# Linear attention on one core: block matrix held stationary, one reciprocal over the whole tile, the low halves of the turned rows on GpSimd

## The chip, the core and the metric

The kernel runs on one core of a Trainium2 chip. The metric is the device time of one execution in microseconds (us), taken as the median over runs of the same kernel.

## What is computed

Four stages act one after another on x of shape (8, 256, 1024): a linear attention against a context, a feed-forward net with 4-bit weights, an autocorrelation attention and a low-rank layer. The change touches the first stage and what it hands to the second:

```python
def _layernorm(x, axis=-1, eps=1e-05): ...

def _L0_xattn_ref(q, k, v):              # B, C, N = 8, 256, 1024; H = 8 heads of dh = 32
    ...
    qh = jax.nn.softmax(qh, axis=3)      # over the 32 channels of a head
    kh = jax.nn.softmax(kh, axis=1)      # over the 1024 positions
    kvs = jnp.einsum('bnhd,bnhe->bhde', kh, vh)
    out = jnp.einsum('bnhd,bhde->bnhe', qh, kvs)
    return out.transpose(0, 2, 3, 1).reshape(B, C, N)

x = x + jnp.tanh(g_xattn[0]) * _L0_xattn_ref(_layernorm(x, axis=-1), ctx_4096, ctx_4096)
x = x + jnp.tanh(g_ffn[0]) * _L0_ffn_ref(_layernorm(x, axis=-1), ...)
```

## The kernel before

The first stage is `phase_linear_attention`. It works on 16 tiles, each of 128 rows (channels) by 1024 columns (positions), in float32; a tile holds four heads of 32 rows. All 16 tiles of x stay in the tile X. Each engine has a program of its own, written out by hand: a function `step(i, h)` that is run for i from 0 to 18, with `exists` leaving out what lies before the first or behind the last tile. The engines are tied by semaphores alone, and most buffers are double (index h). An instruction that waits holds back all that stands behind it on its engine.

For tile i the work is this.

- VectorE (`prepare`) takes the mean and variance of the rows of X and the maximum of the context rows; GpSimd (`rsqrt`, lines 389 to 394) makes the reciprocal root from the variance, and VectorE the offset (line 538).
- ScalarE makes the exponentials of the queries (line 419, eq) and of the keys (line 425, ek).
- TensorE turns ek with eight transposes into psE (line 488), and sums eq over the 32 rows of each head into psB (line 494): there the data are the stationary operand and the block matrix blk, of ones in four 32 by 32 blocks, is the moving one, so psB holds the sums turned, and each sum 32 times. VectorE takes the reciprocal of every 32nd column, 32 in all (line 562, rS). ScalarE spreads them over 1024 columns into rSx (line 454), TensorE turns that back into psB (line 512), ScalarE copies psB to rSx (line 461), and GpSimd multiplies eq by it (line 401).
- ScalarE copies the turned keys (line 448, ekT), TensorE multiplies them with the context (line 507), VectorE masks and scales the product (line 579, kvm), TensorE multiplies with eq (line 501, psO), and VectorE adds the result to X (line 567). This last pair is done one step later, at step i + 1.
- Still at step i + 1, VectorE takes mean and variance of the new row of X (line 530), GpSimd the root, and ScalarE writes the normalised rows to xn (line 471). xn lies in two buffers, one of `wt` and one of `absm`.
- At step i + 2 TensorE turns xn into psX (line 518) and ScalarE writes its high half in 16 bits to z (line 430, `turned_high`). At step i + 3 VectorE writes the low half, psX minus the high half (line 552, `turned_low`).

ScalarE also does a part of the next phase's weight decoding between these (line 442). The end of the phase has a small chain of scales for the feed-forward net (`ffn_scales`), run for the last steps: its power on GpSimd is line 200. After the phase all engines meet, and the feed-forward net begins.

Of the kernel before, what the change touches and what calls it, by code (L numbers as in the profile page):

```python
# [22 lines left out]
ALU = mybir.AluOpType  # L23
# [3 lines left out]
P = 128  # L27
# [258 lines left out]
def phase_linear_attention(nc, io, res):  # L286
# [9 lines left out]
    with ExitStack() as ctx:  # L296
# [7 lines left out]
        c_in, cT, eq, ek, ekT = (sb(n, [P, D]) for n in ("c_in", "cT", "eq", "ek", "ekT"))  # L304
        xn = [t.rearrange("p a b -> p (a b)") for t in (res["wt"][:, 2:4, :], res["absm"][:, 0:2, :])]
        spare = parts(res["made"][:].rearrange("p a b -> p (a b)").bitcast(F32))
        kvm, rS, st, st2 = ([spare(n) for h in range(2)] for n in (P, D // ROWS0, 12, 12))
        spare = parts(res["made"][:].rearrange("p a b -> p (a b)").bitcast(F32)[:, 4 * P - 48:])
        mv, mv2, ve, rstd, nmr, ve2, rstd2, nmr2, cm, ncm, ksum, rks = ([spare(n) for h in range(2)] for n in (2, 2, *(1,) * 10))
        rSx = res["wt"][:, 0:2, :].rearrange("p a b -> p (a b)")  # L310
# [6 lines left out]
        mv_done, rstd_done, nmr_done = (sem(n) for n in ("mv_done", "rstd_done", "nmr_done"))  # L317
        cmax_done, ncm_done, eq_done, ek_done, rks_done = (sem(n) for n in ("cmax_done", "ncm_done", "eq_done", "ek_done", "rks_done"))
        ekT_mm, ekT_done, kv_mm, kvm_done = (sem(n) for n in ("ekT_mm", "ekT_done", "kv_mm", "kvm_done"))
        sums_mm, rS_done, rSx_done, rS_mm, eqn_done, out_mm, x_done = (sem(n) for n in ("sums_mm", "rS_done", "rSx_done", "rS_mm", "eqn_done", "out_mm", "x_done"))  # L320
        mv2_done, rstd2_done, nmr2_done = (sem(n) for n in ("mv2_done", "rstd2_done", "nmr2_done"))
        turned_done = sem("turned_done")
        hi_done = res["hi_done"]
# [5 lines left out]
        def halves_of(i, h):  # L329

            b, r = i // 2, i % 2
            return x_tiles(res, b // QUARTS)[:, :, r, b % QUARTS, h]

        def turned_bank():
            return psX[:].rearrange("p (f k t) -> p f k t", f=2, k=KD // 2)
# [12 lines left out]
        with nc.Block() as block:  # L348
# [38 lines left out]
            @block.gpsimd  # L387
            def _(pool):
                def rsqrt(i, h, mv_, ve_, rs_, mvd, rsd):
                    pool.wait_ge(mvd, 3 * i + 3)  # L390
                    settle(pool)
                    pool.tensor_scalar(ve_[h][:], mv_[h][:, 1:2], EPS, None, ALU.add).then_inc(rsd, 1)
                    pool.wait_ge(rsd, 2 * i + 1)
                    pool.tensor_tensor(rs_[h][:], ve_[h][:], mhalf[:], ALU.pow).then_inc(rsd, 1)

                def step(i, h):
                    if exists(i - 1):
                        rsqrt(i - 1, 1 - h, mv2, ve2, rstd2, mv2_done, rstd2_done)
                    if exists(i):
                        pool.wait_ge(turned_done, i + 1)  # L400
                        pool.tensor_tensor(eq[h][:], rSx[:], eq[h][:], ALU.mult).then_inc(eqn_done, 1)
                    if exists(i + 2):
                        rsqrt(i + 2, h, mv, ve, rstd, mv_done, rstd_done)

                pool.memset(mhalf[:], -0.5).then_inc(const_set, 1)
                pool.memset(res["half"][:], 0.5).then_inc(const_set, 1)
                pool.memset(res["ones"][:], 1.0).then_inc(const_set, 1)
                pool.wait_ge(const_set, 3)
                for h in range(2):
                    rsqrt(h, h, mv, ve, rstd, mv_done, rstd_done)  # L410
                run(pool, step, scales_pool)

            @block.scalar
            def _(act):
                def query_exponentials(i, h):
                    act.wait_ge(nmr_done, i + 1)
                    after(act, out_mm, i - 1)
                    settle(act)
                    act.activation(eq[h][:], X[:, i, :], ACT.Exp, scale=rstd[h][:], bias=nmr[h][:]).then_inc(eq_done, 1)

                def key_exponentials(i, h):
                    after(act, ekT_mm, i - 1)
                    after(act, rks_done, i - 1)
                    act.wait_ge(ncm_done, i + 1)
                    act.activation(ek[h][:], c_in[h][:], ACT.Exp, bias=ncm[h][:], accum_out=ksum[h][:]).then_inc(ek_done, 1)

                def turned_high(i):
                    act.wait_ge(xT_mm, i + 1)
                    settle(act)
                    act.activation(halves_of(i, 0), turned_bank(), ACT.Copy, scale=LN_SCALE).then_inc(hi_done, 1)  # L430

                def first_kinks(i):

                    turn, k = divmod(i - 1, len(kinks))
                    if 0 <= turn < 2:
                        scale, bias, alpha = kinks[k]
                        act.wait_ge(res["first_in"], 16 * (AHEAD // 2) * (turn + 1))
                        if k:
                            act.wait_ge(res["kink_done"], AHEAD // 2 * (i - 1))
                        for u in range(AHEAD // 2 * turn, AHEAD // 2 * (turn + 1)):  # L440
                            block_u = res["first"][:, u, :]
                            act.activation(block_u, block_u if k else block_u.bitcast(I32), ACT.Prelu, bias=bias, scale=scale, alpha=alpha).then_inc(res["kink_done"], 1)

                def step(i, h):
                    if exists(i):
                        after(act, kv_mm, i - 1)
                        act.wait_ge(ekT_mm, i + 1)
                        act.activation(ekT[h][:], psE[:], ACT.Copy).then_inc(ekT_done, 1)
                    first_kinks(i)
                    if exists(i):  # L450
                        after(act, eqn_done, i)
                        act.wait_ge(rS_done, i + 1)

                        act.activation(rSx[:].rearrange("p (n r) -> p n r", r=ROWS0), rS[h][:].unsqueeze(2).to_broadcast([P, D // ROWS0, ROWS0]),
                                       ACT.Copy).then_inc(rSx_done, 1)
                    if exists(i + 1):
                        query_exponentials(i + 1, 1 - h)
                        key_exponentials(i + 1, 1 - h)
                    if exists(i):
                        act.wait_ge(rS_mm, i + 1)  # L460
                        act.activation(rSx[:], psB[:], ACT.Copy).then_inc(turned_done, 1)
                    if i == 0:
                        act.wait_ge(bound_in, 32)
                        act.activation(tg[:], gates[:], ACT.Tanh).then_inc(tanh_done, 1)
                    if i == TILES:
                        turned_high(i - 2)
                    if exists(i - 1):
                        after(act, xT_mm, i - 2)
                        act.wait_ge(nmr2_done, i)
                        settle(act)  # L470
                        act.activation(xn[1 - h][:], X[:, i - 1, :], ACT.Identity, scale=rstd2[1 - h][:], bias=nmr2[1 - h][:]).then_inc(xn_done, 1)
                    if exists(i - 2) and i != TILES:
                        turned_high(i - 2)

                act.wait_ge(const_set, 2)
                act.activation(rstd2[0][:], res["half"][:], ACT.Exp)
                key_exponentials(0, 0)
                query_exponentials(0, 0)
                run(act, step, scales_act)

            @block.tensor
            def _(pe):
                def step(i, h):
                    if exists(i):
# [3 lines left out]
                            mm = pe.transpose(psE[:, k * P:(k + 1) * P], ek[h][:, k * P:(k + 1) * P], ident[:])  # L488
                        mm.then_inc(ekT_mm, 1)

                        after(pe, turned_done, i)
                        pe.wait_ge(eq_done, i + 1)
                        for k in range(KD):
                            mm = pe.matmul(psB[:, k * P:(k + 1) * P], eq[h][:, k * P:(k + 1) * P], blk[:], start=True, stop=True)
                        mm.then_inc(sums_mm, 1)
                    if exists(i - 1):
                        pe.wait_ge(eqn_done, i)
# [5 lines left out]
                    if exists(i):  # L503
# [3 lines left out]
                            mm = pe.matmul(psE[:, 0:P], ekT[h][:, k * P:(k + 1) * P], cT[h][:, k * P:(k + 1) * P], start=(k == 0), stop=(k == KD - 1))  # L507
                        mm.then_inc(kv_mm, 1)

                        pe.wait_ge(rSx_done, i + 1)  # L510
                        for k in range(KD):
                            mm = pe.transpose(psB[:, k * P:(k + 1) * P], rSx[:, k * P:(k + 1) * P], ident[:])
                        mm.then_inc(rS_mm, 1)
                    if exists(i - 2):
                        pe.wait_ge(xn_done, i - 1)
                        after(pe, lo_done, i - 2)
                        for k in range(KD):
                            mm = pe.transpose(psX[:, k * P:(k + 1) * P], xn[h][:, k * P:(k + 1) * P], ident[:])
                        mm.then_inc(xT_mm, 1)
# [5 lines left out]
            def _(dve):  # L525
# [21 lines left out]
                    dve.wait_ge(cmax_done, i + 1)  # L547
                    dve.tensor_scalar(ncm[h][:], cm[h][:], -1.0, None, ALU.mult).then_inc(ncm_done, 1)

                def turned_low(i):  # L550
                    dve.wait_ge(hi_done, i + 1)
                    dve.scalar_tensor_tensor(halves_of(i, 1), turned_bank(), LN_SCALE, halves_of(i, 0), ALU.mult, ALU.subtract).then_inc(lo_done, 1)

                def step(i, h):
                    if exists(i - 3) and i != TILES + 1:
                        turned_low(i - 3)
                    if exists(i):
                        dve.wait_ge(ek_done, i + 1)
                        dve.reciprocal(rks[h][:], ksum[h][:]).then_inc(rks_done, 1)
                        dve.wait_ge(sums_mm, i + 1)  # L560

                        dve.reciprocal(rS[h][:], psB[:, 0:D:ROWS0]).then_inc(rS_done, 1)
                    if exists(i - 1):
                        dve.wait_ge(out_mm, i)
                        if i == 1:
# [5 lines left out]
                        stats(i - 1, 1 - h, st2, mv2, mv2_done)  # L571
                        if i == TILES:
                            scales_dve(dve, "every")
                            turned_low(i - 2)
                    if exists(i):
                        dve.wait_ge(rks_done, i + 1)
                        dve.wait_ge(kv_mm, i + 1)
# [2220 lines left out]
```

## Time and profile before

| | |
|---|---|
| median of 3 runs | 1982.77 us (1982.44 to 1983.53) |
| profiled execution, own time | 1984.28 us |
| its span, first to last instruction | 1982.5 us |
| TensorE busy in the span | 1925.9 us, 97% |
| VectorE, ScalarE, GpSimd busy | 1268.0, 1248.0, 822.3 us |
| mean granted TensorE clock | 0.992 |
| linear attention phase | the first 176 us or so |

The page gives busy times for the whole span; what the change can do has to be read from the phase that it touches. That phase repeats one pattern per tile, so two neighbouring steps of the timeline, and the start of the same instruction in each, give the length of a step. In the rows a tile that lies in another's memory bears that one's name: `made` holds the small vectors (statistics, offsets, rS, kvm), `wt` holds rSx and one of the two xn, `absm` the other xn, `z` the turned halves. PEld is the loading of weights into TensorE. A float32 matmul appears as two matmul records.

### The profile page before, as it was taken

How to read it: one execution, taken by the hardware profiler on the slowest of the kernel's cores; microseconds unless marked ns; L12 is line 12 of the kernel's file. 1: busy time of each engine (PE TensorE's matmuls, PEld its weight loads, DVE VectorE, ACT ScalarE, POOL GpSimd, SP SyncE). 2: the span in 40 equal slices, each digit the busy share in tenths (PEclk: the TensorE clock that was granted, in tenths of full speed). 3: DMA queues.
4: the chain of work that ended last, by engine and by line, in shares of the span. 5: the costliest groups of instructions: out<-in, count | busy, mean ns of one | idle time of the engine just before them, and what ended most of it. 6: DMA issues, size and time to landing. Idle time of an engine off the chain costs nothing. (4 is left out here: it accounts for less than half of the span.)

```text
span 1982.5 us, 26463 instructions
## 1 busy us (share of the span) xinstructions
PE 1925.9 (97%) x9188; PEld 969.2 (49%) x9188; DVE 1268.0 (64%) x2184; ACT 1248.0 (63%) x1989; POOL 822.3 (41%) x746
## 2 busy tenths in 40 slices
PE   7996999999999999999999999999999899999998
PEld 6773444444444444444444444444444455555544
DVE  6776666573645747365463745546389888888872
ACT  6885888667876777676777767765534444344431
POOL 3433644532222232232322323222278667767742
PEclk9997999999999999999999999999999999999999
DMA  6641733248566383765737465562551110111001
GB/s 222 204 164 54 245 99 96 104 169 284 196 212 233 113 279 110 241 202 168 262 102 269 145 222 200 159 246 77 202 165 32 33 53 24 47 54 38 27 22 43
DMA packets 89972, 288.33 MB, mean 145 GB/s; under 512 B 11760, under 2 KB 16496, under 8 KB 72944
## 3 DMA queue, kind: packets, MB, share of 16 engines
q1 hardware_dynamic: 89840, 286.64, 42.8%
q8 instruction: 74, 1.21, 0.3%
q14 instruction: 58, 0.48, 0.1%
HBM read 259.33 MB, written 27.26 MB: 145 GB/s over the span
## 5 line engine op out<-in xcount | busy, mean ns | idle before, releaser
L1050 ACT ACTIVATE first<-first 128x512 f32<-128x512 f32 (+1 forms) x1024 | 635.9, 626 | 26.3 <-DVE wt L1459 1.8
L1284 POOL TENSOR_TENSOR gu<-wt,gu 128x512 f16<-128x512 f32 x86 | 102.5, 1192 | 389.5 <-ACT gu L1071 389.5
L1459 DVE SCALAR_TENSOR_TENSOR wt<-first,w_scale,absm 128x512 f32<-128x512 f32 x132 | 102.3, 775 | 237.8 <-ACT first L1050 237.3
L1806 PE MATMUL a_psQ<-z,gu 128*128 128x512 f16 x840 | 187.2, 379 | 0.0
L2409 PE MATMUL a_psL<-z,l_x 128*128 128x512 f16 x768 | 170.7, 379 | 1.0 <-DVE l_x L2511 0.8
L1806 PE MATMUL a_psC<-z,gu 128*128 128x512 f16 x660 | 151.3, 379 | 0.0
L1806 PE MATMUL a_psC<-z 128*128 128x512 f16 x612 | 140.4, 379 | 0.0
L1462 DVE SCALAR_TENSOR_TENSOR wt<-a_psE,lora_gain,wt 128x512 f32<-128x512 f32 x132 | 99.1, 751 | 54.0 <-PE a_psE L1764 26.9
L1806 PEld LDWEIGHTS a_psQ<-z,gu 128*128 128x128 f16 x840 | 82.2, 98 | 99.1
L1284 POOL TENSOR_TENSOR dn_lo<-wt,dn_hi 128x512 f16<-128x512 f32 x42 | 49.0, 1167 | 192.1 <-ACT dn_hi L1071 192.1
L1296 POOL TENSOR_TENSOR hid_lo<-z,hid_hi 128x512 f16<-128x512 f32 x68 | 80.6, 1199 | 109.7 <-ACT hid_hi L1112 109.6
L1071 ACT ACTIVATE gu<-wt 128x512 f16<-128x512 f32 x86 | 53.5, 622 | 105.1 <-DVE wt L1462 81.3
L2409 PEld LDWEIGHTS a_psL<-z,l_x 128*128 128x128 f16 x768 | 74.9, 98 | 89.0 <-issue 1.2
L1521 DVE SCALAR_TENSOR_TENSOR X<-a_psL,ffn_gain,X 128x512 f32<-128x512 f32 x132 | 95.3, 745 | 24.5 <-PE a_psL L1863 24.4
L1284 POOL TENSOR_TENSOR z<-wt,z 128x512 f16<-128x512 f32 x51 | 59.8, 1188 | 103.2 <-ACT z L1071 103.2
L1863 PE MATMUL a_psL<-dn_hi,hid_hi 128*128 128x512 f16 x268 | 101.6, 379 | 0.2 <-DVE X L1521 0.2
L1863 PE MATMUL a_psL<-dn_hi,hid_lo 128*128 128x512 f16 x268 | 101.5, 379 | 0.0
L1521 DVE SCALAR_TENSOR_TENSOR X<-a_psQ,ffn_gain,X 128x512 f32<-128x512 f32 x106 | 77.7, 746 | 36.6 <-PE a_psQ L1863 36.6
L1806 PEld LDWEIGHTS a_psC<-z,gu 128*128 128x128 f16 x660 | 63.8, 98 | 74.2
L1521 DVE SCALAR_TENSOR_TENSOR X<-a_psC,ffn_gain,X 128x512 f32<-128x512 f32 x108 | 78.8, 746 | 32.6 <-PE a_psC L1863 32.6
L1863 PE MATMUL a_psL<-dn_lo,hid_hi 128*128 128x512 f16 x254 | 96.2, 379 | 0.0
L1806 PEld LDWEIGHTS a_psC<-z 128*128 128x128 f16 x612 | 59.5, 98 | 70.5
(421 smaller groups left out, 4180.5 us busy)
## 6 DMA issues: line engine op xcount, KB each, us to landing
z<-x_parts SPq DMA_DIRECT2D x126, 1024.0 KB, 5.8
first<-in_codes SPq DMA_DIRECT2D x132, 256.0 KB, 3.1
absm<-in_absmax SPq DMA_DIRECT2D x264, 128.0 KB, 3.4
c_in<-in_ctx SPq DMA_DIRECT2D x16, 512.0 KB, 5.1
X<-in_x SPq DMA_DIRECT2D x16, 512.0 KB, 4.8
cT<-in_ctxT SPq DMA_DIRECT2D x16, 512.0 KB, 3.5
o_sp<-in_w SPq DMA_DIRECT2D x16, 512.0 KB, 4.4
z<-in_ctx SPq DMA_DIRECT2D x8, 1024.0 KB, 7.2
```

The source lines that it names most:

```text
L1050: act.activation(level[w % 2][:], codes[w % RING] if k == 0 else level[w % 2][:], ACT.Prelu, bias=bias, scale=scale, alpha=alpha).then_inc ...
L1071: act.activation(dest(c, name, 0), wt[slot(name)], ACT.Copy).then_inc(whi_done, 1)
L1284: pool.tensor_tensor(low, source, high, ALU.subtract).then_inc(wlo_done, 1)
L1296: pool.tensor_tensor(low, buf, high, ALU.subtract).then_inc(hidlo_done, 1)
L1459: dve.scalar_tensor_tensor(wt[at], source[:], w_scale[:, m:m + 1], absm[w % RING][:], ALU.mult, ALU.mult).then_inc(scaled, 1)
L1462: dve.scalar_tensor_tensor(wt[at], ps_lora[w % 2], lora_gain[:, m:m + 1], wt[at], ALU.mult, ALU.add).then_inc(wt_done, 1)
L1521: dve.scalar_tensor_tensor(dst, ps_ring[down_bank(j, n)], ffn_gain[:], dst, ALU.mult, ALU.add).then_inc(acc_done, 1)
L1806: mm = pe.matmul(out, w[:, k * P:(k + 1) * P], xx[:, k], start=first and q == 0, stop=q == 3 * KD // 2 - 1, skip_group_check=True)
L1863: mm = pe.matmul(ps_ring[down_bank(j, n)], hh[c][:, i * P:(i + 1) * P], w[c][:, hf * BANK:(hf + 1) * BANK], start=(q == 0), stop=(q == len ...
L2409: mm = pe.matmul(sum_bank(d, half), a[:, ks], w[:, k, half * CB:(half + 1) * CB], start=(q == 0), stop=(q == 3 * KD - 1))
```

## The change

The matmuls at line 494 become two matmuls of 512 columns, with blk stationary and eq moving, so that psB holds the sums in the layout of eq. VectorE takes the reciprocal of all 1024 columns of psB straight into rSx, and GpSimd multiplies by that. The 32 column reciprocal, ScalarE's spreading, the eight transposes and ScalarE's copy fall away. The turned rows are first copied by ScalarE from psX into the memory of xn (`turned_rows`); ScalarE then makes the high half from this copy, and the low half becomes a subtraction on GpSimd of operands in SBUF, at the end of GpSimd's step. The wait ahead of writing xn (line 468) is now for the low half of the tile that used this buffer before, and no longer for its transposes.

```diff
@@ gpsimd
+                def turned_low(i):
+                    pool.wait_ge(hi_done, i + 1)
+                    pool.tensor_tensor(halves_of(i, 1), turned_rows(i), halves_of(i, 0), ALU.subtract).then_inc(lo_done, 1)
+
                 def step(i, h):
                     if exists(i - 1):
                         rsqrt(i - 1, 1 - h, mv2, ve2, rstd2, mv2_done, rstd2_done)
                     if exists(i):
-                        pool.wait_ge(turned_done, i + 1)
+                        pool.wait_ge(rS_done, i + 1)
                         pool.tensor_tensor(eq[h][:], rSx[:], eq[h][:], ALU.mult).then_inc(eqn_done, 1)
                     if exists(i + 2):
                         rsqrt(i + 2, h, mv, ve, rstd, mv_done, rstd_done)
+                    if exists(i - 3):
+                        turned_low(i - 3)
@@ scalar
                 def turned_high(i):
                     act.wait_ge(xT_mm, i + 1)
                     settle(act)
-                    act.activation(halves_of(i, 0), turned_bank(), ACT.Copy, scale=LN_SCALE).then_inc(hi_done, 1)
+                    act.activation(turned_rows(i), turned_bank(), ACT.Copy, scale=LN_SCALE).then_inc(turned_done, 1)
+                    act.wait_ge(turned_done, i + 1)
+                    act.activation(halves_of(i, 0), turned_rows(i), ACT.Copy).then_inc(hi_done, 1)
...
-                    if exists(i):
-                        after(act, eqn_done, i)
-                        act.wait_ge(rS_done, i + 1)
-
-                        act.activation(rSx[:].rearrange("p (n r) -> p n r", r=ROWS0), rS[h][:].unsqueeze(2).to_broadcast([P, D // ROWS0, ROWS0]),
-                                       ACT.Copy).then_inc(rSx_done, 1)
                     if exists(i + 1):
                         query_exponentials(i + 1, 1 - h)
                         key_exponentials(i + 1, 1 - h)
-                    if exists(i):
-                        act.wait_ge(rS_mm, i + 1)
-                        act.activation(rSx[:], psB[:], ACT.Copy).then_inc(turned_done, 1)
...
                     if exists(i - 1):
-                        after(act, xT_mm, i - 2)
+                        after(act, lo_done, i - 2)
@@ tensor
-                        after(pe, turned_done, i)
+                        after(pe, rS_done, i)
                         pe.wait_ge(eq_done, i + 1)
-                        for k in range(KD):
-                            mm = pe.matmul(psB[:, k * P:(k + 1) * P], eq[h][:, k * P:(k + 1) * P], blk[:], start=True, stop=True)
+                        for n in range(2):
+                            mm = pe.matmul(psB[:, n * BANK:(n + 1) * BANK], blk[:], eq[h][:, n * BANK:(n + 1) * BANK], start=True, stop=True)
                         mm.then_inc(sums_mm, 1)
...
-                        pe.wait_ge(rSx_done, i + 1)
-                        for k in range(KD):
-                            mm = pe.transpose(psB[:, k * P:(k + 1) * P], rSx[:, k * P:(k + 1) * P], ident[:])
-                        mm.then_inc(rS_mm, 1)
                     if exists(i - 2):
                         pe.wait_ge(xn_done, i - 1)
-                        after(pe, lo_done, i - 2)
+                        after(pe, turned_done, i - 2)
@@ vector
-                def turned_low(i):
-                    dve.wait_ge(hi_done, i + 1)
-                    dve.scalar_tensor_tensor(halves_of(i, 1), turned_bank(), LN_SCALE, halves_of(i, 0), ALU.mult, ALU.subtract).then_inc(lo_done, 1)
-
                 def step(i, h):
-                    if exists(i - 3) and i != TILES + 1:
-                        turned_low(i - 3)
                     if exists(i):
                         dve.wait_ge(ek_done, i + 1)
                         dve.reciprocal(rks[h][:], ksum[h][:]).then_inc(rks_done, 1)
                         dve.wait_ge(sums_mm, i + 1)
 
-                        dve.reciprocal(rS[h][:], psB[:, 0:D:ROWS0]).then_inc(rS_done, 1)
+                        after(dve, eqn_done, i)
+                        dve.reciprocal(rSx[:], psB[:]).then_inc(rS_done, 1)
...
                             scales_dve(dve, "every")
-                            turned_low(i - 2)
```

## Rows read from the trace of the kernel before

**Rows 1.** The page: busy time of each engine, share of the span, instructions
```profile
PE 1925.9 (97%) x9188; PEld 969.2 (49%) x9188; DVE 1268.0 (64%) x2184; ACT 1248.0 (63%) x1989; POOL 822.3 (41%) x746
```

**Rows 2.** Stretches: us, busy PE, PEld, DVE, ACT, POOL, granted clock, DMA share, GB/s
```profile
70.00:80.00 10.00, 9.22 (x64) 7.38 (x63) 7.92 (x16) 8.53 (x11) 3.91 (x5) 1.00 0.49 161
160.00:165.00 5.00, 2.84 (x4) 1.29 (x5) 3.27 (x7) 2.75 (x4) 2.10 (x1) 0.66 0.00 0
250.00:1982.00 1732.00, 1715.30 (x7902) 821.42 (x7900) 1097.04 (x1863) 1057.55 (x1734) 715.14 (x624) 1.00 0.42 141
```

**Rows 3.** Timeline, one step: start us, us, engine, line, op [idle before]
```profile
60.23 0.16 DVE L538 SCALAR_TENSOR_TENSOR made<-made 128x1 f32<-128x1 f32 x1 [0.79 <-POOL made L394]
60.37 1.22 DVE L552 SCALAR_TENSOR_TENSOR z<-psX,z 128x1024 f16<-128x1024 f32 x1
61.57 0.34 DVE L562 RECIPROCAL made<-psB 128x32 f32<-128x32 f32 x1
61.83 1.19 DVE L567 SCALAR_TENSOR_TENSOR X<-psO,tg,X 128x1024 f32<-128x1024 f32 x1
62.00 1.06 ACT L454 ACTIVATE wt<-made 128x1024 f32<-128x1024 f32 x1 [1.04 <-DVE made L562]
62.97 1.23 ACT L419 ACTIVATE eq<-X,made 128x1024 f32<-128x1024 f32 x1
64.59 0.21 DVE L533 BATCH_NORM_AGGREGATE made<-made 128x2 f32<-128x12 f32 x1
65.23 1.00 ACT L461 ACTIVATE wt<-psB 128x1024 f32<-128x1024 f32 x1
65.30 0.57 POOL L394 TENSOR_TENSOR made<-made,mhalf 128x1 f32<-128x1 f32 x1
65.47 1.06 PE L488 MATMUL psE<-ident,ek 128*128 128x128 f32 x8 [0.39 <-ACT ek L425]
65.90 0.16 DVE L538 SCALAR_TENSOR_TENSOR made<-made 128x1 f32<-128x1 f32 x1 [0.84 <-POOL made L394]
66.17 1.24 ACT L471 ACTIVATE wt<-X,made 128x1024 f32<-128x1024 f32 x1
66.31 2.36 POOL L401 TENSOR_TENSOR eq<-wt,eq 128x1024 f32<-128x1024 f32 x1 [0.44 <-ACT wt L461]
66.37 1.97 PE L494 MATMUL psB<-blk,eq 128*128 128x128 f32 x16
67.58 1.17 DVE L545 TENSOR_REDUCE made<-c_in 128x1 f32<-128x1024 f32 x1
68.73 1.98 PE L501 MATMUL psO<-eq,made 128*128 128x512 f32 x4 [0.39 <-POOL eq L401]
69.12 1.14 ACT L442 ACTIVATE first<-first 128x512 f32<-128x512 f32 x2
69.55 0.16 DVE L538 SCALAR_TENSOR_TENSOR made<-made 128x1 f32<-128x1 f32 x1 [0.80 <-POOL made L394]
```

**Rows 4.** Line 562 alone: count, ns min/median/max, first and last start us
```profile
L562 DVE RECIPROCAL made<-psB x16: 336/340/358, 15.2 to 153.5; 128x32 f32<-128x32 f32 x16
```

**Rows 5.** Groups by shape, VectorE: busy us, mean ns, idle before
```profile
L2573 DVE RECIPROCAL rws<-wsum 128x4 f32<-128x4 f32 x15 | 2.7, 178 | 0.5
L559 DVE RECIPROCAL made<-made 128x1 f32<-128x1 f32 x16 | 2.5, 154 | 0.0
L235 DVE COPY absm<-psB 128x12 f32<-128x12 f32 x1 | 0.1, 115 | 0.0
```

**Rows 6.** Groups by shape, GpSimd and ScalarE, for the moved work
```profile
L1284 POOL TENSOR_TENSOR gu<-wt,gu 128x512 f16<-128x512 f32 x86 | 102.5, 1192 | 389.5 <-ACT gu L1071 389.5
L1040 ACT ACTIVATE lora_a<-gain_row,ab_scale 96x1024 f16<-96x1024 f32 x1 | 1.1, 1131 | 0.0
```

**Rows 7.** Timeline, the end of the phase
```profile
159.75 2.36 POOL L401 TENSOR_TENSOR eq<-wt,eq 128x1024 f32<-128x1024 f32 x1 [0.97 <-ACT wt L461]
162.16 3.40 PE L501 MATMUL psO<-eq,made 128*128 128x512 f32 x4 [2.68 <-POOL eq L401]
```

More of the change, by code:

```diff
@@ L306, in phase_linear_attention @@
         spare = parts(res["made"][:].rearrange("p a b -> p (a b)").bitcast(F32))
-        kvm, rS, st, st2 = ([spare(n) for h in range(2)] for n in (P, D // ROWS0, 12, 12))
+        kvm, st, st2 = ([spare(n) for h in range(2)] for n in (P, 12, 12))
         spare = parts(res["made"][:].rearrange("p a b -> p (a b)").bitcast(F32)[:, 4 * P - 48:])
@@ L319, in phase_linear_attention @@
         ekT_mm, ekT_done, kv_mm, kvm_done = (sem(n) for n in ("ekT_mm", "ekT_done", "kv_mm", "kvm_done"))
-        sums_mm, rS_done, rSx_done, rS_mm, eqn_done, out_mm, x_done = (sem(n) for n in ("sums_mm", "rS_done", "rSx_done", "rS_mm", "eqn_done", "out_mm", "x_done"))
+        sums_mm, rS_done, eqn_done, out_mm, x_done = (sem(n) for n in ("sums_mm", "rS_done", "eqn_done", "out_mm", "x_done"))
         mv2_done, rstd2_done, nmr2_done = (sem(n) for n in ("mv2_done", "rstd2_done", "nmr2_done"))
@@ L332, in halves_of, with turned_rows @@
             return x_tiles(res, b // QUARTS)[:, :, r, b % QUARTS, h]
+        def turned_rows(i):
+            return xn[i % 2].rearrange("p (f k t) -> p f k t", f=2, k=KD // 2)
         def turned_bank():
```

## The prediction, made before the changed kernel had run

> **What bounds the kernel now.** I read the busy times first, then the stretches, then one step of the timeline. TensorE is busy 97% of the span [rows 1]. From 250 us on it works 1715 of 1732 us at the full clock of 2.4 GHz [rows 2]. The change touches none of that, only the first 176 us, and all engines meet at their end, so what the phase gains or loses shifts the rest as it is. In the phase no engine is full: of 10 us PE works 9.2, ScalarE 8.5, VectorE 7.9 and GpSimd 3.9 [rows 2]. The step is set by a ring. VectorE's offset comes at 60.23 and again at 69.55: a step is 9.32 us. Follow it in [rows 3]: offset, low half (60.37), 32 column reciprocal (61.57), ScalarE's spreading (62.00), the exponentials (62.97), the copy back (65.23), GpSimd's product (66.31 to 68.67), the root behind it, the next offset. The reader should see the short idle times in brackets: 1.04 on ScalarE, 0.44 on GpSimd, 0.80 and 0.84 on VectorE. All are waits for the ring's last link.
>
> **What the change takes out.** Out of the ring go the spreading (1.06), the copy back (1.00) and the low half on VectorE (1.22), and ScalarE's exponentials no longer stand between reciprocal and product. ScalarE loses 2.06 us a step and gets one copy more, about 1.0 by line 461 [rows 3]. TensorE loses eight transposes, 1.06 us by line 488. Its sums keep their price: two 512 column products were 1.98 us (line 501), the sixteen records of line 494 were 1.97 [rows 3]. If neither engine is the bound, this is worth nothing.
>
> **What it puts in: the full reciprocal.** No row shows a reciprocal of 1024 columns, so its duration R is bounded by shorter ones. 32 columns take 340 ns [rows 4], 4 take 178 and 1 takes 154 [rows 5]. From 1 to 32 columns that is 186/31 = 6.0 ns a column, so R = 0.15 + 1023 x 0.006 = 6.3 us. With the fixed part of the small copy out of PSUM (115 ns for 12 columns, some 103 without them) it is 237/32 = 7.4 ns and R = 7.7. From 1 to 4 columns it is 8 ns, and R = 8.3. If half of the 340 ns were a cost of the strided read, 5.3 ns would be left and R = 5.5. The lowest bound is a whole-tile operation of VectorE of another kind, 1.17 to 1.19 us (lines 545, 567) [rows 3]; it would need some 0.31 us fixed in the 32 column form, and the one column form takes half of that altogether. I take R = 6.5, near the slope over the widest span.
>
> By the Trainium skill (VectorE: DVE Perf Modes, under Walkthrough: the 8-slice pipeline in each mode, on the fixed hardware budget), a reciprocal is an iterated divide with a repeat count of 8, while in the regular mode there is one result a cycle. Eight cycles at the skill's 0.96 GHz are 8.3 ns a column, an estimate of R = 8.7 us; one cycle would be an estimate of 1.2. The slope from 1 to 4 columns agrees with eight, that to 32 columns lies below it [rows 4, 5].
>
> **The VectorE ring with R.** A step of 9.32 less its two waits (0.84, 0.80) is 7.68 of work in starts. The low half takes 1.15 of it (60.37 to 61.57 less a small reciprocal) and the old reciprocal 0.26 (61.57 to 61.83), so 6.3 stay. The 0.84 stays: statistics, root, offset are as before. The product can now start when this root ends (65.87) and not at 66.31, so the other wait falls to 0.4. The step is 6.3 + 0.84 + 0.4 + R = 7.5 + R: 14.0 us for R = 6.5. It breaks even at R = 1.8.
>
> **The moved low half and its new wait.** GpSimd gets 2 x 1.19 = 2.4 us a step [rows 6], behind its product and the second root. It has idle time for that. But ScalarE's xn of tile i-1 now waits for the low half of tile i-3, that is for the end of GpSimd's whole step i. Queued behind this wait on ScalarE are both copies of the turned rows, ekT, the decoding, and the next two exponentials; TensorE's sums and so the reciprocal wait for these. That makes a second ring, over two steps [rows 3]: R; addition to statistics 2.97 (61.83 to 64.80); root 1.07; product 2.42; second root 0.88; low half 2.4; xn, high half, ekT and decoding 4.09 (66.17 to 70.26) plus 1.1 for the extra copy (a 96 row conversion from SBUF took 1.13 [rows 6]); exponentials up to the key transposes 2.50 (62.97 to 65.47); transposes and sums 2.87 (65.47 to 68.34); some 0.1 of hand-over. Together 20.4 + R, a step of 10.2 + R/2. With R = 6.5 it is 13.45, just under the first ring; below R = 5.4 it takes over, and at R = 1.2 it still gives 10.8, above 9.32.
>
> **TensorE's clock.** Its work, 9.32 x 0.92 less 1.06 = 7.5 us a step [rows 2, 3], no longer fills 14. Counting from a reciprocal's start, the product before ends at -1.0, psO at +0.9, and the next key-context product waits for ekT, at about 6.5: idle for 5.5 us. In the trace, after 2.68 us idle, line 501 took 3.40 us in place of 1.98 [rows 7, 3], in a stretch with a granted clock of 0.66, part of it at 1.2 GHz [rows 2]. Slowed 1.72 times, line 507 and the turned rows (about 3.0) end near 11.7, transposes and sums near 14.7, 0.7 late; since a longer step also moves the start, half of that counts, 0.35. With all four at the low clock it is 1.45. Over 14 steps the clock costs 0 to 20 us; I take 7. The Trainium skill (TensorE: Matmul & The Clock Gate, Part 1) says the clock is set by how busy TensorE has been; the row agrees.
>
> **The sum.** From first to last reciprocal there were 138.3 us (15.2 to 153.5) in 15 intervals [rows 4]. Now 14 are 14.0; the last has no preparation in front of it (65.90 to 69.55, 3.4 without the part of the wait that is gone), so 10.6: 206.6, or +68.3. From the last reciprocal to its product were 6.25 (153.5 to 159.75 [rows 7]), now R + 2.97 + 1.07 = 10.5: +4.3. Behind it a low half stands ahead of the last xn and of the scales' power on GpSimd (+2.4), one copy more (+1.1), and the last low half is 2.4 in place of 1.2 (+1.2): +4.7. With the clock 68.3 + 4.3 + 4.7 + 7 = +84. The profiled execution took 1984.3 of its own, with a span of 1982.5; +84 gives 2068.6, and against the median, 1.5 lower, 2067.
>
> **The rivals.**
> - *A dearer reciprocal or a low clock throughout.* R = 8.3 gives 15.8 a step, 16 x 1.8 = 29 more, less the clock's 7, as TensorE has slack again: 2089. The low clock alone: 2067 + 13 = 2080.
> - *A cheaper one.* With R = 4.2 the second ring holds at 12.3: 14 x 1.7 + 2 x 2.3 + 4 of the clock less, 2035. For R from 5.5 it is 2051 and up, my own case.
> - *The reciprocal runs at a column a nanosecond and the new wait on ScalarE takes its place.* 14 x 10.8 + 10 - 138.3 = +23, the last product -1, the tail +4.7: 2010. For it speaks that every other whole-tile operation runs so; against, the 340 ns.
> - *Not slower, but faster.* R under 1.8, and the second ring is shorter than the rows make it, because ScalarE gets ahead early and GpSimd's low half is done in time. Then the first ring holds at 8.7: 15 x -0.6 + 4.7 - 1, 1977. It needs both; the second ring would have to lose 3 us.
>
> **How the numbers follow.** My case 0.60 (2050 to 2080), dearer or low clock 0.14, R near 4 0.07, the ScalarE wait 0.14, faster 0.04, within 0.2% (about what a measurement of this kernel can tell from no change) 0.01. The range 2030 to 2095 leaves out the last three, 0.19.
>
> **What would show it.** The full reciprocal's group has a mean of 5.5 to 7.7 us; VectorE is busy some 12.8 of each 14 us from 30 to 200, with idle ahead of line 538 only; reciprocals start 14 us apart; GpSimd's low halves take 2.4; ScalarE waits ahead of xn for GpSimd for over 3 us; TensorE idles 5 us a step, with a granted clock below 1. A mean near 1.2 proves the main term wrong, and the step then tells which ring holds.

## The result and the profile after

The changed kernel takes 2105.11 us in the median of 4 runs (2104.57 to 2105.84), the kernel before 1982.61 us (1981.21 to 1983.53): a ratio of 1.0619, 95% interval 1.06 to 1.0637. It is 122.5 us slower. The forecast was 84 us slower, 2067 us, with a range up to 2095; the time lies 10 us above the range.

First the page of the changed kernel, to be read against [rows 1], and two stretches against [rows 2]:

```profile
PE 1940.0 (92%) x8868; PEld 962.9 (46%) x8868; DVE 1405.4 (67%) x2168; ACT 1234.5 (59%) x1973; POOL 855.0 (41%) x762
```

```profile
100.00:120.00 20.00, 11.66 (x53) 8.81 (x53) 18.55 (x18) 8.55 (x12) 5.98 (x6) 0.76 0.22 79
320.00:2103.00 1783.00, 1763.74 (x8148) 843.84 (x8146) 1131.76 (x1901) 1099.39 (x1806) 749.41 (x652) 1.00 0.43 144
```

Behind the phase TensorE works as closely as before. In the phase VectorE is now busy 18.55 of 20 us, and TensorE 11.66. VectorE's work in the whole span has grown by 137 us. Its groups by shape, in the first 300 us (busy us, mean ns, idle before), show by what:

```profile
L555 DVE RECIPROCAL wt<-psB 128x1024 f32<-128x1024 f32 x16 | 104.6, 6537 | 2.3 <-PE psB L496 2.3
L536 DVE SCALAR_TENSOR_TENSOR made<-made 128x1 f32<-128x1 f32 x32 | 59.8, 1869 | 14.9 <-POOL made L397 14.6
```

The reciprocal is what was forecast: 6.54 us a tile. The second row was in no term of the sum. It is VectorE's offset, one value a row (minus the mean times the root), which took 0.16 us before [rows 3] and now takes 1.87 in the mean. One step of the timeline (start, us, engine, line) shows when:

```profile
104.07 2.35 POOL L408 TENSOR_TENSOR eq<-wt,eq 128x1024 f32<-128x1024 f32 x1
104.14 2.29 DVE L536 SCALAR_TENSOR_TENSOR made<-made 128x1 f32<-128x1 f32 x1 [0.85 <-POOL made L397]
106.36 1.27 DVE L528 BATCH_NORM_STATS2 made<-X 128x6 f32<-128x512 f32 x2
109.03 2.12 POOL L401 TENSOR_TENSOR z<-wt,z 128x1024 f16<-128x1024 f32 x1
109.09 2.07 DVE L536 SCALAR_TENSOR_TENSOR made<-made 128x1 f32<-128x1 f32 x1
111.22 6.53 DVE L555 RECIPROCAL wt<-psB 128x1024 f32<-128x1024 f32 x1
111.29 1.24 ACT L473 ACTIVATE wt<-X,made 128x1024 f32<-128x1024 f32 x1 [10.15 <-POOL z L401]
115.49 3.78 PE L509 MATMUL psE<-cT,ekT 128*128 128x128 f32 x16 [7.03 <-ACT ekT L459]
121.67 2.35 POOL L408 TENSOR_TENSOR eq<-wt,eq 128x1024 f32<-128x1024 f32 x1
```

From product to product it is 17.60 us; 14.0 were forecast. The steps are this long eleven times; the first three were 11.3, 15.7 and 15.7 us from reciprocal to reciprocal, and the last 12.9. Each time GpSimd starts the product or the low half 0.05 to 0.07 us ahead of the offset, the offset ends with it and not before: 104.07 + 2.35 = 106.42 against 104.14 + 2.29 = 106.43. The profile counts the held time as busy, so no wait shows it. Of the 32 offsets 27 are held, 14 by the product and 13 by the low half; together with the five free ones they are the 59.8 us, where 5 would be the work.

### The profile page after: what moved, and what is told of

The parts are those of the page before. It is cut to its first block and busy times, and to the rows that moved or that the text cites. A ratio compares the mean times of both kernels' runs of the same rounds, so it can differ in the third digit from the quotient of the medians.

```text
span 2103.0 us, 25807 instructions
## 1 busy us (share of the span) xinstructions
PE 1940.0 (92%) x8868; PEld 962.9 (46%) x8868; DVE 1405.4 (67%) x2168; ACT 1234.5 (59%) x1973; POOL 855.0 (41%) x762
## 5 line engine op out<-in xcount | busy, mean ns | idle before, releaser
L509 PE MATMUL psE<-cT,ekT 128*128 128x128 f32 x256 | 52.5, 389 | 82.6 <-ACT ekT L459 82.6
L555 DVE RECIPROCAL wt<-psB 128x1024 f32<-128x1024 f32 x16 | 104.6, 6537 | 2.3 <-PE psB L496 2.3
```

The costliest lines, as they stand in the source:

```text
L555: dve.reciprocal(rSx[:], psB[:]).then_inc(rS_done, 1)
```

## The experiments

All times are medians, beside runs of the kernel before on the same chip (1982 to 1983 us). The theory after the result: VectorE's offset is held by GpSimd whenever both read from SBUF and the offset reads two tensors there; that is the missing 38 us. "Held" means that the instruction starts but doesn't end before GpSimd's. The rival: a small VectorE instruction is held by any GpSimd instruction, or the length has another cause in the changed order.

**The offset with one tensor operand.**

```diff
-                    dve.scalar_tensor_tensor(nm_[h][:], mv_[h][:, 0:1], -1.0, rs_[h][:], ALU.mult, ALU.mult).then_inc(nmd, 1)
+                    dve.tensor_scalar(nm_[h][:], mv_[h][:, 0:1], rs_[h][:], -1.0, ALU.mult, ALU.mult).then_inc(nmd, 1)
```

> The changed kernel, with the row offset on VectorE (line 536) written as a tensor_scalar: the mean is its only tensor operand, the root is a per-row scalar read through a pointer. Theory A (VectorE is held while GpSimd reads SBUF whenever an instruction reads two TENSORS from SBUF): the two stretches of 2.29 and 2.07 us in line 536 shrink to 0.16, the step falls from 17.6 to about 14.0 us and the time by 14 to 15 steps of 3.6, to some 2053 us. Theory B (any second read from SBUF counts, the pointer scalar too, as line 262 hints: a tensor_scalar of 128x3 that took 1.97 us in the changed kernel while GpSimd's low half ran): the step stays at 17.6 and the time at 2105.

Measured: 2064.37 us, ratio 1.0413 (1.0382 to 1.0443), 40.7 us less than the changed kernel. The timeline of this run:

```profile
109.48 2.36 POOL L408 TENSOR_TENSOR eq<-wt,eq 128x1024 f32<-128x1024 f32 x1
109.55 0.21 DVE L536 TENSOR_SCALAR made<-made 128x1 f32<-128x1 f32 x1 [0.47 <-POOL made L397]
112.66 2.12 POOL L401 TENSOR_TENSOR z<-absm,z 128x1024 f16<-128x1024 f32 x1
112.72 0.21 DVE L536 TENSOR_SCALAR made<-made 128x1 f32<-128x1 f32 x1 [0.33 <-POOL made L397]
112.99 6.54 DVE L555 RECIPROCAL wt<-psB 128x1024 f32<-128x1024 f32 x1
```

GpSimd starts 0.07 us ahead as before, and the offset takes 0.21. Theory A holds for one column, and B falls. The reciprocals come 13.97 us apart (99.02 to 112.99): the step of the forecast (14.0), with a time 3 us below its 2067. Against the 2053 expected here it is a miss by 11 us: I had counted 14 to 15 steps with two holds, and there were eleven.

**Mean times root on GpSimd, a negation on VectorE.**

```diff
+                    pool.wait_ge(rsd, 3 * i + 2)
+                    pool.tensor_tensor(nm_[h][:], mv_[h][:, 0:1], rs_[h][:], ALU.mult).then_inc(rsd, 1)
...
+                    dve.tensor_scalar(nm_[h][:], nm_[h][:], -1.0, None, ALU.mult).then_inc(nmd, 1)
```

> The changed kernel, with mean times root computed on GpSimd right behind the root, and VectorE left with a negation by an immediate, one operand from SBUF. Both theories on the shared reads (A and B) expect the negation to take 0.15 us even while GpSimd runs its product or its low half: step 7.5 + 6.5 + some 0.3 for the longer chain on GpSimd = 14.3 us, time near 2058. The rival, that line 536 is long because a small VectorE instruction cannot start or end while GpSimd works, whatever it reads, expects 2 us in the negation and 2105 to 2110.

Measured: 2068.51 us, 10 us more than expected, in steps of 14.4.

```profile
111.13 2.36 POOL L410 TENSOR_TENSOR eq<-wt,eq 128x1024 f32<-128x1024 f32 x1
111.21 0.15 DVE L538 TENSOR_SCALAR made<-made 128x1 f32<-128x1 f32 x1 [0.69 <-POOL made L399]
```

A small instruction is not held as such; this rival is out.

Both edits changed the kind of the instruction with its operands. The trace of before, from the feed-forward net, tells these apart: line 1459 is a `scalar_tensor_tensor` of two tensors in SBUF, line 1462 the same instruction with one in PSUM.

```profile
L1459 DVE SCALAR_TENSOR_TENSOR wt<-first,w_scale,absm x132: 734/745/1647, 179.9 to 1417.5; 128x512 f32<-128x512 f32 x132
L1462 DVE SCALAR_TENSOR_TENSOR wt<-a_psE,lora_gain,wt x132: 750/751/752, 180.7 to 1418.3; 128x512 f32<-128x512 f32 x132
183.60 1.80 POOL L1284 TENSOR_TENSOR gu<-wt,gu 128x512 f16<-128x512 f32 x1 [0.29 <-ACT gu L1071]
184.42 1.53 DVE L1459 SCALAR_TENSOR_TENSOR wt<-first,w_scale,absm 128x512 f32<-128x512 f32 x1
219.42 1.49 POOL L1336 TENSOR_TENSOR o_sp<-o_sp,z 128x512 f32<-128x512 f32 x1
219.93 0.75 DVE L1462 SCALAR_TENSOR_TENSOR wt<-a_psE,lora_gain,wt 128x512 f32<-128x512 f32 x1
```

Started beside a running GpSimd instruction, the first takes 1.53 us in place of 0.75, the second its 0.75 all the same, and none of its 132 is over 0.752. So it is the second tensor in SBUF and not the kind of instruction. But not every GpSimd instruction holds. At the end of the phase its power of 12 columns (line 200), which reads two tensors in SBUF too, starts ahead of the unchanged offset:

```profile
169.91 2.28 POOL L200 TENSOR_TENSOR absm<-absm,half 128x12 f32<-128x12 f32 x1
169.97 0.16 DVE L538 SCALAR_TENSOR_TENSOR made<-made 128x1 f32<-128x1 f32 x1
```

Why it doesn't hold the offset was not tried. The theory stands for the product, the low half and the long operations of the next phase.

**GpSimd waits until the offset is written.**

```diff
                         pool.wait_ge(rS_done, i + 1)
+                        after(pool, nmr2_done, i)
...
+                    if exists(i + 2):
+                        pool.wait_ge(nmr_done, i + 3)
+                    elif exists(i - 1):
+                        pool.wait_ge(nmr2_done, i)
                     if exists(i - 3):
                         turned_low(i - 3)
```

> The changed kernel with two waits added on GpSimd and nothing else: the product of tile i waits until VectorE has written the offset of tile i-1, the low half until it has written the offset of tile i+2. If VectorE's offset is held by a GpSimd instruction that started just before it, then waiting for some 0.2 us on GpSimd takes away 2 x 2 us on VectorE: step 14.0 to 14.2 us, time 2055 to 2060. If the held time has another cause, the step stays at 17.6 or gets longer: 2105 to 2110.

Measured: 2069.70 us, 35 us less, by two waits and no other edit. That is 10 us more than the upper end expected. The steps are mostly 14.3 to 14.8: I had not counted that the product now also stands behind kvm, which VectorE does ahead of the offset.

```profile
110.75 0.16 DVE L541 SCALAR_TENSOR_TENSOR made<-made 128x1 f32<-128x1 f32 x1 [0.17 <-POOL made L397]
111.06 2.36 POOL L409 TENSOR_TENSOR eq<-wt,eq 128x1024 f32<-128x1024 f32 x1 [0.34 <-DVE made L541]
```

The instruction is the unchanged one with two tensors, and takes 0.16 when GpSimd starts behind it. So, for this pair, it is the order of the starts that decides.

**GpSimd's long instructions in halves.**

```diff
-                        pool.tensor_tensor(eq[h][:], rSx[:], eq[h][:], ALU.mult).then_inc(eqn_done, 1)
+                        pool.tensor_tensor(eq[h][:, 0:BANK], rSx[:, 0:BANK], eq[h][:, 0:BANK], ALU.mult)
+                        pool.tensor_tensor(eq[h][:, BANK:D], rSx[:, BANK:D], eq[h][:, BANK:D], ALU.mult).then_inc(eqn_done, 1)
```

and the same for the low half.

> The changed kernel with each of GpSimd's two long operations a step (product and low half, 1024 columns) cut into two of 512 columns; nothing else. If VectorE's offset is held for exactly as long as the GpSimd instruction that had started before it, the two held stretches fall from 2.29 and 2.07 to 1.2 and 1.0 to 1.1 us, the step from 17.6 to about 15.4, the time to some 2078. If the offset is held until GpSimd has nothing more to do, it stays 2.3 and 2.1 and the time near 2105.

Measured: 2078.26 us, steps of 15.56, as the first case expected.

```profile
113.40 1.27 POOL L409 TENSOR_TENSOR eq<-wt,eq 128x512 f32<-128x512 f32 x1
113.46 1.22 DVE L538 SCALAR_TENSOR_TENSOR made<-made 128x1 f32<-128x1 f32 x1 [0.85 <-POOL made L397]
117.28 1.15 POOL L401 TENSOR_TENSOR z<-absm,z 128x512 f16<-128x512 f32 x1
117.34 1.10 DVE L538 SCALAR_TENSOR_TENSOR made<-made 128x1 f32<-128x1 f32 x1
```

Half the instruction holds the offset half as long, 1.22 and 1.10 in place of 2.29 and 2.07. The hold lasts for one GpSimd instruction, and VectorE is done before the second half has run.

**The sums part alone**, with high and low half as before (the edits of the turned rows are taken back).

> Only the sums part of the change: block matrix stationary and full reciprocal, while the low half is again made by VectorE out of psX, as before. With the shared reads: the product starts right behind the root and holds the first offset for 2.2 us, the second offset is free; step 6.3 of the remaining work + 1.15 low half + 0.84 + 2.2 + 6.45 = 16.9 us, time near 2092. Without it (if the two long instructions came from the low half alone): 6.3 + 1.15 + 0.84 + 0.4 + 6.45 = 15.1, time near 2065.

Measured: 2095.89 us, steps of 16.82. The offset's line in this run (count, ns min/median/max, first and last start):

```profile
L528 DVE SCALAR_TENSOR_TENSOR made<-made x32: 158/160/2301, 9.9 to 284.4; 128x1 f32<-128x1 f32 x32
```

The median of 160 ns and the maximum of 2301 are the two kinds of offset: the one behind the product is held, the other, with no low half on GpSimd beside it, is free. Fifteen of the 32 are held. The step is as expected (16.9), the time 4 us over, and this part alone costs 114 us.

**The turned part alone**, on the kernel before.

> Only the turned part of the change: the kernel before with the second copy on ScalarE and the low half on GpSimd; sums, small reciprocal, spreading and copy back as before. Here the new wait closes a ring within ONE step: product 2.4, root 0.9, low half 2.1, xn 1.2, two copies 2.0, ekT 0.9, decoding 1.15, spreading 1.0, two exponentials 2.3, copy back 1.0, together 15 us, since the next product waits for the copy back, which stands behind xn on ScalarE. Expected 15 us a step from the fourth on and about 2055. The rival, that GpSimd's idle time hides the low half and only ScalarE's extra copy counts, expects 9.6 to 10 us a step and 1988 to 1994.

Measured: 2066.56 us, steps of 15.0 to 16.3, 12 us more than expected, and far from the rival.

```profile
112.94 2.12 POOL L407 TENSOR_TENSOR z<-wt,z 128x1024 f16<-128x1024 f32 x1
113.00 2.07 DVE L557 SCALAR_TENSOR_TENSOR made<-made 128x1 f32<-128x1 f32 x1 [2.67 <-POOL made L403]
115.20 1.24 ACT L488 ACTIVATE wt<-X,made 128x1024 f32<-128x1024 f32 x1 [5.51 <-POOL z L407]
```

ScalarE stands 5.51 us ahead of xn and then has the whole rest of its step before it, the copy back last. The ring within one step holds; what was missing in my sum is the copy back's own wait for the transposes of the reciprocals (1.10 and 1.33 us in two neighbouring steps), which stand behind a key-context product that took 3.78 us in place of 1.95 at TensorE's lower clock. The 13 held offsets of this run lie off this ring: what follows them is needed only 5 us later. The two parts cost 114 and 84 us alone and 122 together. They are no sum, since the longer of the two rings sets the step: to the 16.82 us of the sums part the turned part adds its hold of 1.9 and takes off the low half of 1.15 on VectorE, 17.6 as measured.

**A copy in the place of the reciprocal**, which leaves the reciprocal out of the computation, first with the two added waits:

```diff
-                        dve.reciprocal(rSx[:], psB[:]).then_inc(rS_done, 1)
+                        dve.tensor_copy(rSx[:], psB[:]).then_inc(rS_done, 1)
```

> The changed kernel with the two added waits on GpSimd, and with a plain copy of psB into rSx in the place of the full reciprocal: the reciprocal is left out of the computation, so what is multiplied in are the sums themselves. VectorE's own ring would then be 7.5 + 1.2 = 8.7 to 9.0 us a step. The theory that the moved low half makes a second ring over two steps (20.4 + R) expects 10.8 to 11.1 us a step, ScalarE waiting ahead of xn for GpSimd's low half with TensorE's sums behind it, and about 2017 us. The rival, that the new wait on ScalarE costs nothing once the reciprocal is cheap, expects 9 us a step and 1982 to 1986.

Measured: 2044.73 us, 28 more than expected, and a step of 14.4 us, as long as with the reciprocal. 5.3 us less a tile on VectorE had moved the step by nothing; the 25 us less in the whole come from ahead of the first product (6 us) and from the next three steps, which take 9.0 to 10.0 us before the ring closes. Was it the added wait or a ring I had not seen? The next run is the same without the waits and with the pointer form.

> The changed kernel with the offset's root read through a pointer (so that it isn't held) and a plain copy of 1.2 us in the place of the full reciprocal; the reciprocal is left out, the sums themselves are multiplied in. Without the two extra waits of the run e3_copy_wait. If the ring seen there (14.4 us) came from the added wait of the product, the step now falls to the two-step ring's 10.8 and the time to some 2015. If it is a ring within one step, kvm, offset, statistics of tile i+2 on VectorE, their root and then the low half on GpSimd, xn, two copies and ekT on ScalarE, the key-context product on TensorE, kvm of the next tile, it is 0.34 + 0.1 + 1.6 + 0.9 + 2.1 + 1.2 + 2.1 + 0.95 + 1.95 + 0.4 = 11.6 us at TensorE's full clock and 13.4 with that product at the low clock (3.78): 2025 to 2045. In either case the changed kernel without its reciprocal stays slower than the kernel before.

Measured: 2026.54 us, inside the second case's 2025 to 2045. From low half to low half it is mostly 13.1 to 13.4 us, so the added wait had cost about 1 of the 14.4. One turn of the ring, from low half to low half:

```profile
99.35 2.12 POOL L401 TENSOR_TENSOR z<-wt,z 128x1024 f16<-128x1024 f32 x1
101.61 1.24 ACT L473 ACTIVATE wt<-X,made 128x1024 f32<-128x1024 f32 x1 [5.87 <-POOL z L401]
104.76 1.00 ACT L459 ACTIVATE ekT<-psE 128x1024 f32<-128x1024 f32 x1
105.81 3.43 PE L509 MATMUL psE<-cT,ekT 128*128 128x128 f32 x16 [4.46 <-ACT ekT L459]
109.36 0.35 DVE L571 SCALAR_TENSOR_TENSOR made<-psE,made,blk 128x128 f32<-128x128 f32 x1 [4.89 <-PE psE L509]
111.57 0.22 POOL L395 TENSOR_SCALAR made<-made 128x1 f32<-128x1 f32 x1 [3.71 <-DVE made L531]
112.42 2.12 POOL L401 TENSOR_TENSOR z<-absm,z 128x1024 f16<-128x1024 f32 x1
114.69 1.24 ACT L473 ACTIVATE absm<-X,made 128x1024 f32<-128x1024 f32 x1 [5.63 <-POOL z L401]
```

Low half, xn, copies, ekT, key-context product, kvm, statistics and root of the tile after next, low half: 13.07 us, within one step. The idle times in brackets name the links between the engines. So a changed kernel with a reciprocal of 1.2 us and no held offset would still be 44 us slower than before. Of this ring 3.43 is TensorE's key-context product, mostly at the lower clock (granted 0.66 from 105 to 110 us; 1.95 in the kernel before); what the ring is with a full clock was not run.

**The reciprocal as exp(-ln(sum)) on ScalarE**, on the sums part alone:

```diff
+                        act.activation(rSx[:], psB[:], ACT.Ln).then_inc(ln_done, 1)
+                        act.wait_ge(ln_done, i + 1)
+                        act.activation(rSx[:], rSx[:], ACT.Exp, scale=-1.0).then_inc(rS_done, 1)
```

> Sums part alone, with the reciprocal made by ScalarE as exp(-ln(sum)) in place of VectorE's: two operations of 1.0 and 1.2 us take the place of spreading and copy back; small reciprocal, eight transposes and full reciprocal are gone, the low half is on VectorE as before. ScalarE has 8.6 us of work a step, TensorE 7.5. If the product now starts while VectorE's offset is due, the offset is held for 2 us as in the changed kernel: 9.3 to 10.5 us a step, 1983 to 2000. If not, ScalarE is the bound with 8.6 to 8.9 us: 1972 to 1978.

> The kernel of the run before with mean times root computed on GpSimd, so that VectorE's offset reads one operand and can't be held. Expected: ScalarE is the bound, 8.6 to 9.0 us a step, and 1972 to 1979, below the kernel before. Rival: the ring through GpSimd (product, root, mean times root) stays at 9.3 or above, and the time at 1982 or more.

Measured: 2024.88 and 2013.24 us. Both are slower than the kernel before and outside the ranges of the theory; the second lies where its rival put it (1982 or more), but not by the rival's ring. The groups by shape of the first run, ScalarE:

```profile
L457 ACT ACT_TABLE_LOAD x16 | 20.5, 1283 | 0.3
L459 ACT ACT_TABLE_LOAD x16 | 20.5, 1283 | 0.3
```

The two functions each bring a table load of 1.28 us, 2.6 us a tile, on an engine that had some 1 us to spare: in the second run the steps are 11.2 us in the mean, the expected 8.6 and 2.6, and ScalarE is busy 121.8 of the 124 us from 66 to 190. In the first run seven offsets are held, one in every second step, which adds 15 us to them. That run is 11.6 us longer than the second; as the second also has more work on GpSimd, the 11.6 are not the price of the hold alone.

**A faster kernel.** Two runs on the kernel before: the pointer form alone, and with it the low half on VectorE moved behind the small reciprocal.

```diff
-                    if exists(i - 3) and i != TILES + 1:
-                        turned_low(i - 3)
                     if exists(i):
...
                         dve.reciprocal(rS[h][:], psB[:, 0:D:ROWS0]).then_inc(rS_done, 1)
+                    if exists(i - 3) and i != TILES + 1:
+                        turned_low(i - 3)
```

> The kernel BEFORE with the offset's root read through a pointer, and nothing else. In the trace of before one offset alone is held (2.30 us at 28.46), in the first steps. Expected: that one is gone, the ring of 9.32 stays, time 0 to 2 us lower than before: 1981 to 1983.

> The kernel before with the pointer form, and with VectorE's low half moved from ahead of the small reciprocal to right behind it. This takes 1.15 us out of the ring of before (offset, low half, small reciprocal, spreading, exponentials, copy back, product, root); the new limits are ring 9.0 over the addition, statistics and root, and TensorE's 8.6 us of work. Expected 8.8 to 9.0 us a step and 1974 to 1978; with the old form of the offset the product would come early and hold it. Rival: addition and statistics now stand behind the low half and the root comes as late as the copy back did, so nothing is gained: 1981 to 1983.

Measured: 1982.26 us, ratio 0.9996 (0.9986 to 1.0006), and 1975.91 us, ratio 0.9972 (0.9963 to 0.9981). The first can't be told from the kernel before; the second, as expected, is faster, by 6.8 us, so the gain comes with the moved low half. Its timeline:

```profile
63.28 2.36 POOL L401 TENSOR_TENSOR eq<-wt,eq 128x1024 f32<-128x1024 f32 x1
63.35 0.21 DVE L538 TENSOR_SCALAR made<-made 128x1 f32<-128x1 f32 x1 [0.85 <-POOL made L394]
66.78 0.34 DVE L560 RECIPROCAL made<-psB 128x32 f32<-128x32 f32 x1
67.04 1.16 DVE L552 SCALAR_TENSOR_TENSOR z<-psX,z 128x1024 f16<-128x1024 f32 x1
```

The step is 8.93 us in place of 9.32. The product now starts as soon as the root is there, 0.07 us ahead of the offset; with two tensors the offset would be open to the hold here. That combination was not run.

## Why the prediction was wrong, step by step

- **The price of the reciprocal** held: 6.54 us measured, 6.5 taken, from the slope between 1 and 32 columns [rows 4, 5]. That is 6.4 ns a column. The repeat count of 8 that the Trainium skill gives (VectorE: DVE Perf Modes, First, the fixed hardware budget), taken as eight cycles a column, was an estimate of 8.3 and too high.
- **The VectorE ring** is the step that failed, in the sentence "The 0.84 stays ... so the other wait falls to 0.4. The step is 6.3 + 0.84 + 0.4 + R". It moved the product from 66.31 to 65.87, that is from behind the offset at 65.90 to just ahead of it, and took nothing for the change of order. The 0.44 us that GpSimd had waited for the copy back in [rows 3] had kept the two apart. In place of this step the runs showed a held offset: 2.1 us more at the first one and, with the low half right behind the second root, 1.9 more at the second, while the second wait of 0.4 went: 14.0 + 2.1 + 1.9 - 0.4 = 17.6, as measured. The ring itself was right: without the hold it is 13.97, though its idle times are 0.28 for TensorE's key-context product, 0.47 and 0.33 in place of 0.84 and 0.4.
- **The row that would have told** was in the trace before. VectorE's line 538 had a mean of 227 ns over 32, with 160 as its median, and one instance in the first steps, where the product came early:

```profile
28.46 2.30 DVE L538 SCALAR_TENSOR_TENSOR made<-made 128x1 f32<-128x1 f32 x1 [0.85 <-POOL made L394]
```

- The Trainium skill states the rule (SBUF — State Buffer, Who interferes with whom): a VectorE instruction with two SBUF inputs contends with a GpSimd instruction that reads SBUF, and the order of issue decides which of the two is blocked. The traces agree for the long operations: 2.29 us behind a product of 2.35, 1.22 behind one of 1.27. They don't for line 200, whose 2.28 us left the offset at 0.16. The rule spoke against this change and belonged among the rivals; the only rule for VectorE that I had weighed was the one on the divide.
- **The second ring** was named, with the right wait, but mis-traced. I led it through exponentials and sums over two steps and got 10.8 us for R = 1.2; the way through the key-context product, kvm and the next statistics closes within one step, and was 13.1 to 13.4. The rival's 2010 us was too low: the copy run gave 2026.5. In the changed kernel ScalarE waits 10 us for the low half [10.15 in the timeline above], and VectorE sets the end all the same.
- **TensorE's clock** fell as said (granted 0.76 from 100 to 120 us, line 509 at 3.78 us). I took 7 us for it. In the changed kernel VectorE idled 2.3 us in all for the sums, at the first two tiles, and 3.1 for one key-context product: the longer step hides the clock. Without the hold these are 7.2 and 6.8 us, but first to last reciprocal is then 209.4 us where the terms without the clock made 206.6, so some 3 of the 7 show. No run had the full clock throughout, so its price stands alone in none.
- **The ends of the phase** came near: from the last reciprocal to its product +4.2 us (4.3 forecast), from there to line 1459 of the next phase (1451 in the changed kernel) +6.2 (4.7 forecast), with two small instructions of the scales in it that took 2.08 and 1.97 us beside a low half (lines 239 and 262). With the offset's hold gone (the pointer run) the whole is 82.3 us over before by the medians, with 84 forecast. In the traces it is 79.6: 71.1 from first to last reciprocal (68.3 and 7 of the clock forecast), 4.2, 5.8 at the end, and 1.6 less in the rest of the kernel. So the nearness is in part luck.
- **The sum**: first to last reciprocal 249.2 us (15.7 to 264.9) where 206.6 were forecast, +43; the clock's 7 were not spent, which leaves 36. The other 2 of the 38 us are mostly that the profiled execution of before took 1.7 us more than its median.
- The range failed because its upper end was made of prices for the terms I had, and no case stood for an instruction that gets longer through its neighbour.

## What to carry to other kernels

Where an edit lets GpSimd start sooner, look at which VectorE instruction starts next, and count the tensors that it reads from SBUF: with two, a 0.16 us instruction on the ring can cost what the GpSimd instruction costs. Compare mean and median of small instructions in the trace of before; one long instance among short ones is a price list. A moved operation is priced by all the queues that its new waits hold up, and of the ways back round to it the one with the most time for each step that it spans is the ring that counts.

## What the runs showed of the hardware

- A reciprocal of 1024 columns on VectorE takes 6.54 us, a copy of the same tile out of PSUM 1.2.
- A one-column `scalar_tensor_tensor` with two SBUF tensors is held for a GpSimd `tensor_tensor` that started ahead of it, and the hold is shown as busy time: 2.29 us behind a product of 2.35, 2.07 behind a low half of 2.12. A `tensor_tensor` of three columns (line 239) is held alike, 2.08 us in place of 0.16. With the second operand as a pointer scalar it takes 0.21 us and is not held. Open is line 262, a `tensor_scalar` of three columns with such a scalar: it took 1.97 us beside a low half, in the changed kernel and in the pointer run, and 0.23 before. Line 259, a `tensor_scalar` of two columns with a constant, took 0.16 beside the same low half. What sets these apart was not tried, nor why the power of line 200 holds nothing.
- Ln and Exp in turn on ScalarE cost a table load of 1.28 us each time.
